# A four-layer attention and feed-forward kernel: giving up TensorE's products of the identity in banks that wait for their operands

## The chip, the cores and the metric

The kernel runs on one core of one Trainium2 chip. The metric is the time of one execution on the device in microseconds (us), from the runs of the whole program: 1483.53 us is the median of three runs before the change (1482.13 to 1483.54). Engines are named as in the profile: PE is TensorE (its weight loads are shown apart, as PEld), DVE is VectorE, ACT is ScalarE, POOL is GpSimd and SP is SyncE.

## The reference

The input is `x`, 32 sequences of 128 tokens by 128 channels, and a context of 77 rows by 128 channels for each sequence. Eight blocks follow each other, each added to the residual of a layer-normed input:

```python
x = x + _L0_xattn_ref(_layernorm(x), ctx_1024, ctx_1024, ...)   # 16 heads of 8
x = x + _L0_ffn_ref(_layernorm(x), ...)                         # 8 heads of 64, gated experts
x = x + _L1_xattn_ref(_layernorm(x), ctx_1024, 32, ...)         # the 32 largest scores of 77
x = x + _L1_ffn_ref(_layernorm(x), ...)                         # causal attention, then 8 experts, 2 chosen
x = x + _L2_xattn_ref(_layernorm(x), ctx_1024)
x = x + _L2_ffn_ref(_layernorm(x), ...)                         # quantised with the largest value of the whole x
x = x + _L3_xattn_ref(_layernorm(x), ctx_1024, ...)             # causal, 16 heads of 8
x = x + _L3_ffn_ref(_layernorm(x), ...)                         # 512 wide
```

All of it is float32, apart from the masks and the quantised products, which are bfloat16. The quantised block needs the largest value of all of `x`, and later the largest of all hidden values, so that the kernel has two points at which nothing can go on before all sequences have been seen.

## The kernel before, in words

The 32 sequences are worked in eight groups (`g`) of four. Phase A does the first five blocks for all groups; phase B the first half of the quantised block; phase C its second half and the last two blocks. In each phase every engine runs several streams of steps side by side: on TensorE of phase A the streams are `x0p`, `x0s`, `x0v` (first attention), `f0p`, `f0s`, `f0t`, `f0v`, `f0o` (first feed-forward), `x1`, `f1p`, `f1s`, `f1t`, `f1v`, `m1` (which holds the experts and the L2 attention), `kv3` and `weights`; of phase C `down`, `x3p`, `x3s`, `x3t`, `x3v` and `f3`. The order in which the streams take turns is written out as one string of letters for each phase and engine (`ORDER`), and `merge` follows it. So each engine's order is fixed when the program is built, and an engine that waits for one step holds up all the steps behind it.

TensorE writes each step's products into a PSUM bank: a ring `E` of four banks of 512 columns and a ring `S` of two pairs of banks of 1024 columns. A step takes the next bank of a ring, waits until whoever read its last contents is through (`drained`), and then waits for its operands: a copy that ACT, DVE or POOL has yet to finish. When its last product is done, the bank's `full` tells the reader.

Between these two waits stands `keep` (line 519). It looks up a digit for this use of this step in the table `FILL` (lines 93 to 151) and issues so many products of the identity with itself, 128 columns wide, into the bank that was just taken. Nobody reads them: the step's own first product starts the bank anew. No semaphore is tied to them.

```python
            def keep(o, step):
                k = uses[step] = uses.get(step, -1) + 1
                for _ in range(int(FILL[step][k])):
                    mm(o.bank[:, 0:128], ident[:], ident[:], start=True, stop=True)
```

A step that uses it, the transposes of `f0o` (from line 692):

```python
                    o = E.take("f0", g, "ys", b)
                    pe.wait_ge(o.drained, o.n)
                    keep(o, "f0o0")
                    pe.wait_ge(f0_ys, C.next(f0_ys))
                    for t in range(3):
                        ins = pe.transpose(o.bank[:, tokens(t)], ys[:, b % 2, tokens(t)], ident[:])
                    ins.then_inc(o.full, 1)
```

`FILL` has 1028 digits, of which 229 are not zero; they add up to 585. In the profile a float32 product stands as two records, so the fills are 1170 records of line 525. Of other lines that the prediction names: L530 is `transpose4`, the transposes of normed activations; L688 the second product of the first feed-forward; L826 the scores of the causal attention and L495 its masks; L840 and L672 transposes; L1197 and L1207 the two products of the last feed-forward; L2265 a product on POOL that ends a layer norm; L1219 ACT's copy out of a bank.

Of the kernel before, what the change touches and what calls it, by code (L numbers as in the profile page):

```python
# [90 lines left out]
        "fddddddfff",  # L91
}
FILL = {
    "down0": "00330000",
    "f0o0": "04000020030140000410001200000330",
    "f0o1": "00020001000010002000000000000001",
    "f0p0": "70700010",
    "f0p1": "00000000000060000000000000000000",
    "f0s0": "0000000000130300000000200001003000001000000220000003000300200000",
    "f0s1": "00000005000000003000100230301030",  # L100
    "f0t0": "2400303000000000400002003210104010001000203010000000020002000000",
    "f0v0": "00111100520002100201000000000602",
    "f1p0": "10020160",
    "f1p1": "0100000030000000",
    "f1p2": "20002040",
    "f1s0": "30000001000000002000200100037000",
    "f1t0": "00004040000000005001400302000030",
    "f1t1": "00000020000000000000000000000000",
    "f1v0": "00100002002033004000122000100333",
    "f1v1": "31012001",  # L110
    "f30": "00100009",
    "f31": "00000000000000001000000121003000",
    "f32": "00000000",
    "kv30": "00000000",
    "kv31": "00000002",
    "m10": "53015040",
    "m11": "00000000",
    "m12": "00400200",
    "m13": "1000000030000000000006203000200000000420000000020001000090000000",
    "m14": "00800027",  # L120
    "m15": "01011304",
    "m16": "10000007",
    "m17": "00000300",
    "m18": "00010008",
    "weights0": "00000001",
    "weights1": "00",
    "weights2": "0",
    "weights3": "0",
    "x0p0": "03000000",
    "x0p1": "00300200",  # L130
    "x0p2": "20000000",
    "x0p3": "00200000",
    "x0s0": "0300000000004300020020000004000000000100000130200010001000000023",
    "x0v0": "00001000300020000002110004002500",
    "x0v1": "00000000",
    "x10": "13000100",
    "x11": "00000010",
    "x12": "20030000",
    "x13": "00300001",
    "x14": "00034020",  # L140
    "x15": "71309100",
    "x16": "10011130",
    "x17": "10020011",
    "x3p0": "50000000",
    "x3p1": "05051300",
    "x3s0": "00000010000000000000000000100000",
    "x3t0": "00232020030000500000300000000200",
    "x3t1": "10000000000000030001000000000000",
    "x3v0": "00000000000100000000000000000000",
    "x3v1": "20000003",  # L150
}


# [2421 lines left out]
```

## Time and profile before

| | before |
|---|---|
| runs | 1483.53 us median of 3 (1482.13 to 1483.54) |
| the profiled execution's own time | 1494.39 us |
| its span, first to last instruction | 1492.6 us |
| granted TensorE clock, mean over the span | 0.916 |
| PE busy, with 16148 records | 1256.4 us (84%) |
| DVE / ACT / POOL busy | 1010.2 / 838.4 / 770.9 us |
| fills (L525): PE busy | 193.1 us, 1170 records |

How to read it: the profiled execution took 10.9 us longer than the median. PE's busy time is a union of records whose ends reach into the next one, so that it is more than the time in which the array works. The granted clock is 1.00 where TensorE runs at 2.4 GHz and 0.50 where it runs at 1.2 GHz; a figure between them is a mixture of the two. The chain of waits is followed back from the last instruction; on this program it reaches back to 758 us and no further, so that its shares of the span add up to about half.

### The profile page before, as it was taken

The numbers are of one execution on the slowest core, as the hardware profiler recorded it, in microseconds if no ns is written. First come the engines' busy times: TensorE is split into PE (matmuls) and PEld (weight loads), VectorE is DVE, ScalarE is ACT, GpSimd is POOL, SyncE is SP. The second block draws the span as 40 slices with busy tenths as digits, with TensorE's granted clock in tenths as the row PEclk, the third lists the DMA queues.
The fourth block names the chain that finished last, engine by engine and source line by source line (L and its number), as shares of the span: only waits on it lengthen the run. The fifth ranks groups of instructions, "written<-read, shape, count | busy, mean of one in ns | idle before, by whom it ended". The sixth has DMA issues, their size and how long they took to land. (4 is left out here: it accounts for less than half of the span.)

```text
span 1492.6 us, 40390 instructions
## 1 busy us (share of the span) xinstructions
PE 1256.4 (84%) x16148; PEld 987.0 (66%) x16149; DVE 1010.2 (68%) x2431; ACT 838.4 (56%) x2675; POOL 770.9 (52%) x793
## 2 busy tenths in 40 slices
PE   4889788878978898898899879889976678999897
PEld 3677677665756677677677757667655157776676
DVE  4357787776877786777668668887654856655562
ACT  3697666445458658658838545563544454444332
POOL 4048487475277419622853763682111677444343
PEclk8598989998989999999989889999998578999999
DMA  6000000000000000000000000001010000000000
GB/s 164 6 2 2 1 1 2 2 2 1 22 1 1 21 2 2 2 22 2 1 21 2 2 1 2 17 1 55 1 54 13 12 2 2 10 10 9 16 10 15
DMA packets 26705, 19.24 MB, mean 13 GB/s; under 512 B 6520, under 2 KB 24216, under 8 KB 26392
## 3 DMA queue, kind: packets, MB, share of 16 engines
q1 hardware_dynamic: 24936, 15.78, 3.6%
q8 instruction: 129, 2.11, 0.6%
q10 hardware_dynamic: 1584, 0.89, 0.2%
q14 instruction: 56, 0.46, 0.1%
HBM read 12.73 MB, written 3.93 MB: 11 GB/s over the span
## 5 line engine op out<-in xcount | busy, mean ns | idle before, releaser
L1219 ACT ACTIVATE arena<-bank 128x512 f32<-128x512 f32 (+5 forms) x363 | 185.8, 546 | 262.4 <-PE bank L530 90.1
L1631 DVE TENSOR_REDUCE arena<-pair 128x8 f32<-128x1024 f32 (+2 forms) x224 | 240.2, 1095 | 113.4 <-PE pair L495 59.8
L2315 POOL TENSOR_TENSOR arena<-arena 128x512 f32<-128x512 f32 x160 | 181.4, 1134 | 79.7 <-DVE arena L1749 72.7
L1266 ACT ACTIVATE arena<-pair,arena 77x128 f32<-77x128 f32 x512 | 178.3, 369 | 23.7 <-DVE arena L1631 16.9
L2320 POOL TENSOR_TENSOR arena<-arena 128x512 f32<-128x512 f32 x128 | 182.1, 1423 | 10.0
L525 PE MATMUL bank<-ident 128*128 128x128 f32 x1008 | 164.7, 299 | 9.8 <-ACT arena L1219 9.4
L525 PEld LDWEIGHTS bank<-ident 128*128 128x128 f32 x1008 | 141.5, 206 | 37.6 <-issue 18.7
L2253 POOL TENSOR_SCALAR arena<-arena 128x4 f32<-128x4 f32 x64 | 21.0, 328 | 276.6 <-DVE arena L1638 225.5
L2336 POOL TENSOR_TENSOR arena<-arena 128x512 f32<-128x512 f32 x64 | 67.4, 1070 | 136.5 <-ACT arena L1219 94.3
L2260 POOL TENSOR_SCALAR_AFFINE_SELECT arena<-arena 77x1024 f32<-77x1024 f32 x64 | 69.7, 1104 | 107.9 <-ACT arena L1603 107.8
L1603 ACT ACTIVATE arena<-pair 77x1024 f32<-77x1024 f32 x64 | 62.8, 1016 | 104.7 <-PE pair L1138 96.6
L1266 ACT ACTIVATION_READ_ACCUMULATOR arena<-pair,arena 77x1 f32 x512 | 107.9, 211 | 0.0
L1219 ACT ACTIVATE arena<-bank,arena 128x128 f32<-128x128 f32 x256 | 75.8, 509 | 40.0 <-PE bank L922 24.7
L1631 DVE TENSOR_REDUCE arena<-arena 128x4 f32<-128x32 f32 (+3 forms) x128 | 70.0, 551 | 37.0 <-ACT arena L1219 26.4
L1326 ACT ACTIVATE arena<-pair,arena 128x128 f32<-128x128 f32 x256 | 90.0, 394 | 7.6 <-DVE arena L1631 7.4
L530 PE MATMUL bank<-ident,arena 128*128 128x128 f32 (+1 forms) x352 | 59.7, 298 | 39.0 <-POOL arena L2265 17.8
L1436 ACT ACTIVATE arena<-pair 128x1024 f32<-128x1024 f32 x64 | 63.0, 1024 | 43.7 <-PE pair L495 41.8
L1784 DVE TENSOR_TENSOR arena<-bank,arena 128x512 f32<-128x512 f32 x96 | 61.3, 681 | 33.2 <-ACT arena L1219 33.1
L580 PE MATMUL pair<-arena 32*77 32x128 f32 x1024 | 74.2, 292 | 11.1 <-ACT arena L1266 9.2
L688 PE MATMUL bank<-arena 128*128 128x64 f32 x512 | 68.7, 293 | 11.4 <-ACT arena L1380 6.2
L688 PEld LDWEIGHTS bank<-arena 128*128 128x128 f32 x512 | 67.0, 210 | 16.1 <-issue 9.3
L580 PEld LDWEIGHTS pair<-arena 32*77 32x77 f32 x1024 | 59.8, 153 | 24.8 <-ACT arena L1266 11.8
(303 smaller groups left out, 2980.0 us busy)
## 6 DMA issues: line engine op xcount, KB each, us to landing
arena<-in_ctx_turned SPq DMA_DIRECT2D x16, 154.0 KB, 2.8
arena<-in_x SPq DMA_DIRECT2D x8, 256.0 KB, 4.4
out<-arena SPq DMA_DIRECT2D x8, 256.0 KB, 2.3
spill<-arena SPq DMA_DIRECT2D x7, 256.0 KB, 2.0
arena<-spill SPq DMA_DIRECT2D x7, 256.0 KB, 4.4
arena<-in_ctx SPq DMA_DIRECT2D x8, 154.0 KB
arena<-in_ctx_turned SPq DMA_DIRECT2D x1, 1232.0 KB, 5.8
wexp<-in_L_ffn_expert_w SPq DMA_DIRECT2D x1, 512.0 KB, 4.2
```

What stands on the lines that cost most here:

```text
L525: mm(o.bank[:, 0:128], ident[:], ident[:], start=True, stop=True)
L580: ins = mm(o[p].bank[0:CTX, 512 * i + 128 * j:512 * i + 128 * j + 128], sub0[rows, b, j, :], q0[rows, tokens(b)], start=True, stop=True)
L688: ins = mm(o.bank[:, h * SHD:(h + 1) * SHD], eF[:, b % 2, 512 * p + 128 * t:512 * p + 128 * t + 128], vs[:, b % 2, h, :], start=True, stop ...
L1219: return act.activation(dst, src, func, bias=bias, scale=scale)
L1266: ins = act.activation(e0[0:CTX, (2 * SEQS * g + u) % 3, tokens(i)], o.bank[0:CTX, tokens(i)], ACT.Exp, bias=negmax0[0:CTX, u, i:i + 1], a ...
L1326: ins = act.activation(pF[:, tokens(i)], o.bank[:, tokens(i)], ACT.Exp, bias=negF[:, b % 2, i:i + 1], accum_out=zF[:, b, i:i + 1])
L1436: act.activation(eG[:, (2 * SEQS * g + u) % 3, :], o.bank[:], ACT.Exp).then_inc(o.drained, 1)
L1631: return dve.tensor_reduce(dst, src, X, op, **kw)
L2260: return pool.affine_select(out=e, in_=e, compare_op=ALU.is_ge, fill=0.0, base=0, pattern=[[0, 8], [1, 128]], channel_multiplier=-1)
L2315: pool.tensor_tensor(into, xvs[:, b, ex * SHD:(ex + 1) * SHD].unsqueeze(1).broadcast_to([128, SH, SHD]), gates[g % 2][:, b, 0:SH, ex].unsq ...
L2320: ins = pool.tensor_tensor(dst, dst, into, ALU.add)
L2336: ins = pool.tensor_tensor(oprod[:, ex, :].rearrange("p (h k) -> p h k", h=SH), av, gates[g % 2][:, b, SH:, ex].unsqueeze(2).broadcast_to( ...
```

## The change

All digits of `FILL` become zero. `keep` is still called and issues nothing; the rings, the waits, the order strings and all other engines' programs are the same.

```diff
 FILL = {
-    "down0": "00330000",
-    "f0o0": "04000020030140000410001200000330",
...
-    "f0s0": "0000000000130300000000200001003000001000000220000003000300200000",
...
-    "f0t0": "2400303000000000400002003210104010001000203010000000020002000000",
...
-    "m13": "1000000030000000000006203000200000000420000000020001000090000000",
...
-    "x0s0": "0300000000004300020020000004000000000100000130200010001000000023",
...
+    "down0": "00000000",
+    "f0o0": "00000000000000000000000000000000",
...
+    "f0s0": "0000000000000000000000000000000000000000000000000000000000000000",
...
+    "f0t0": "0000000000000000000000000000000000000000000000000000000000000000",
...
+    "m13": "0000000000000000000000000000000000000000000000000000000000000000",
...
+    "x0s0": "0000000000000000000000000000000000000000000000000000000000000000",
...
 }
```

The orders of DVE, ACT, POOL and SP do not differ in a single row; TensorE's has 1674 rows before and 1438 after. In the rows that follow, a fill is an L525 row, "bank" and "pair" are the PSUM banks of the two rings, "ident" the identity, "arena" the SBUF area that holds the activations, and x9 stands for nine products of one kind in a row. First, TensorE in phase A, where the causal attention's scores of one sequence are followed by a transpose of another stream. Before:

```order
771 L826 MATMUL pair<-arena 128x256 x8
772 L495 MATMUL pair<-after,identb 32x4x32 x4
773 L495 MATMUL pair<-after,identb 32x4x64 x4
774 L495 MATMUL pair<-after,identb 32x4x96 x4
775 L495 MATMUL pair<-after,identb 32x512 x4
776 L525 MATMUL bank<-ident 128x128 x5
777 L840 MATMUL bank<-ident,arena 128x128 x2
778 L525 MATMUL bank<-ident 128x128
779 L530 MATMUL bank<-ident,arena 128x128 x4
780 L672 MATMUL bank<-ident,arena 128x128 x4
781 L525 MATMUL bank<-ident 128x128
782 L721 MATMUL bank<-arena,w1k 128x308
```

Seven fills stood here in three places between real products; after the change rows 776, 778 and 781 are gone and L840 follows L495 directly.

Second, the end of TensorE's program, where the last group's normed activations are transposed (L530) and go through the last feed-forward (L1197, L1207). The difference of the two orders:

```order
 L1164 MATMUL bank<-arena 32x128 x16
 L1164 MATMUL bank<-arena,onesd 32x128 x16
-L525 MATMUL bank<-ident 128x128 x3
 L1176 MATMUL bank<-arena 128x128 x4
-L525 MATMUL bank<-ident 128x128 x9
-L530 MATMUL bank<-ident,arena 128x128 x4
-L525 MATMUL bank<-ident 128x128 x3
+L530 MATMUL bank<-ident,arena 128x128 x4
 L1197 MATMUL bank<-arena 128x512 x4
 L1207 MATMUL bank<-arena 128x128 x16
```

Fifteen fills leave the last steps; the real products keep their order.

## Rows read from the trace of the kernel before

**Rows 1.** The page's first part, and the granted clock by core.

```profile
PE 1256.4 (84%) x16148; PEld 987.0 (66%) x16149; DVE 1010.2 (68%) x2431; ACT 838.4 (56%) x2675; POOL 770.9 (52%) x793
core 0: 1492.6 us, clock 0.916
```

**Rows 2.** Chain that ended last, by engine, as shares of the whole span.

```profile
PE 30%; DVE 6%; ACT 5%; POOL 4%; issue 3%; POOLq 0%; ACTq 0%; DVEq 0%
```

**Rows 3.** Chain of waits from 758 to 1492.6 us, shares by line.

```profile
by line: PE bank L1164 7.3%; PE bank L525 5.7%; issue 5.6%; PE pair L1138 4.6%; ACT arena L1219 4.3%; PE bank L1207 4.0%; PE bank L1197 3.6%; DVE arena L1631 3.5%; PE pair L1111 2.8%; PE bank L530 2.6%; PE pair L495 2.5%; PE pair L826 2.4%;
```

**Rows 4.** Groups by line: the fills into single banks and into pairs.

```profile
L525 PE MATMUL bank<-ident 128*128 128x128 f32 x1008 | 164.7, 299 | 9.8 <-ACT arena L1219 9.4 <-DVE arena L1906 0.3
...
L525 PE MATMUL pair<-ident 128*128 128x128 f32 x162 | 28.4, 308 | 4.8 <-DVE arena L1631 1.8 <-ACT arena L1266 1.6 <-ACT arena L1436 1.1
```

**Rows 5.** By stretch: us; busy of PE, PEld, DVE, ACT, POOL; PEclk; DMA; GB/s.

```profile
0.00:758.00 758.00, 631.77 (x7106) 506.87 (x7106) 533.99 (x1288) 485.39 (x1855) 424.81 (x431) 0.91 0.05 13
758.00:1492.60 734.60, 624.65 (x9042) 480.10 (x9043) 476.19 (x1144) 352.97 (x820) 346.09 (x363) 0.92 0.04 13
```

**Rows 6.** Busy time by stretch, line 525 alone: PE, PEld, then PEclk.

```profile
0.00:758.00 758.00, 101.88 (x622) 86.77 (x622) 0.91 0.05 13
758.00:1492.60 734.60, 91.21 (x548) 77.95 (x548) 0.92 0.04 13
```

**Rows 7.** Chain of waits from 750 to 770 us, in order of time.

```profile
758.24 2.09 PE pair L826 x16
...
760.91 2.43 PE bank L525 x10
763.35 0.43 PE bank L840 x2
```

**Rows 8.** Timeline at the program's end.

```profile
1474.47 2.17 PE L525 MATMUL bank<-ident 128*128 128x128 f32 x18
...
1478.19 1.04 POOL L2265 TENSOR_TENSOR arena<-arena 128x512 f32<-128x512 f32 x1
...
1479.28 0.65 PE L530 MATMUL bank<-ident,arena 128*128 128x128 f32 x4 [2.64 <-POOL arena L2265]
...
1480.62 3.70 PE L1197 MATMUL bank<-arena 128*128 128x512 f32 x8
...
1485.26 3.81 PE L1207 MATMUL bank<-arena 128*128 128x128 f32 x32 [0.94 <-DVE arena L2175]
```

**Rows 9.** Busy time in short stretches, all engines (columns as in rows 5).

```profile
13.70:17.10 3.40, 2.02 (x13) 1.25 (x12) 0.00 (x0) 1.30 (x4) 3.18 (x3) 1.00 0.73 144
...
212.00:215.00 3.00, 0.60 (x6) 0.41 (x4) 2.93 (x10) 2.89 (x17) 2.92 (x3) 1.00 0.00 0
218.50:222.00 3.50, 3.50 (x20) 3.27 (x21) 3.40 (x17) 0.60 (x1) 3.27 (x4) 0.51 0.00 0
222.00:225.30 3.30, 3.30 (x38) 3.00 (x38) 3.20 (x7) 0.26 (x1) 3.22 (x4) 1.00 0.00 0
...
675.90:679.30 3.40, 2.54 (x23) 2.35 (x22) 3.30 (x9) 2.84 (x16) 0.00 (x0) 1.00 0.00 0
...
1478.00:1481.40 3.40, 2.10 (x12) 1.62 (x13) 0.00 (x0) 0.60 (x1) 2.41 (x3) 1.00 0.00 0
```

**Rows 10.** The same stretches, line 525 alone: PE, PEld, then PEclk.

```profile
13.70:17.10 3.40, 0.61 (x4) 0.53 (x4) 1.00 0.73 144
143.40:146.80 3.40, 1.45 (x7) 1.16 (x6) 0.50 0.00 0
...
218.50:222.00 3.50, 2.45 (x10) 2.25 (x10) 0.51 0.00 0
675.90:679.30 3.40, 2.08 (x18) 1.96 (x18) 1.00 0.00 0
...
1245.90:1249.30 3.40, 1.22 (x4) 0.93 (x4) 0.50 0.00 0
1478.00:1481.40 3.40, 0.83 (x6) 0.75 (x6) 1.00 0.00 0
```

More of the change, by code:

```diff
@@ L93 @@
 FILL = {
-    "down0": "00330000",
-    "f0o0": "04000020030140000410001200000330",
-    "f0o1": "00020001000010002000000000000001",
-    "f0p0": "70700010",
-    "f0p1": "00000000000060000000000000000000",
-    "f0s0": "0000000000130300000000200001003000001000000220000003000300200000",
-    "f0s1": "00000005000000003000100230301030",
-    "f0t0": "2400303000000000400002003210104010001000203010000000020002000000",
[L102 to L112, printed above, removed]
+    "down0": "00000000",
+    "f0o0": "00000000000000000000000000000000",
+    "f0o1": "00000000000000000000000000000000",
+    "f0p0": "00000000",
+    "f0p1": "00000000000000000000000000000000",
+    "f0s0": "0000000000000000000000000000000000000000000000000000000000000000",
+    "f0s1": "00000000000000000000000000000000",
+    "f0t0": "0000000000000000000000000000000000000000000000000000000000000000",
+    "f0v0": "00000000000000000000000000000000",
+    "f1p0": "00000000",
+    "f1p1": "0000000000000000",
+    "f1p2": "00000000",
+    "f1s0": "00000000000000000000000000000000",
+    "f1t0": "00000000000000000000000000000000",
+    "f1t1": "00000000000000000000000000000000",
+    "f1v0": "00000000000000000000000000000000",
+    "f1v1": "00000000",
+    "f30": "00000000",
+    "f31": "00000000000000000000000000000000",
     "f32": "00000000",
     "kv30": "00000000",
-    "kv31": "00000002",
-    "m10": "53015040",
+    "kv31": "00000000",
+    "m10": "00000000",
     "m11": "00000000",
-    "m12": "00400200",
-    "m13": "1000000030000000000006203000200000000420000000020001000090000000",
[L120 to L125, printed above, removed]
+    "m12": "00000000",
+    "m13": "0000000000000000000000000000000000000000000000000000000000000000",
+    "m14": "00000000",
+    "m15": "00000000",
+    "m16": "00000000",
+    "m17": "00000000",
+    "m18": "00000000",
+    "weights0": "00000000",
     "weights1": "00",
@@ L128 @@
     "weights3": "0",
[L129 to L132, printed above, removed]
-    "x0s0": "0300000000004300020020000004000000000100000130200010001000000023",
-    "x0v0": "00001000300020000002110004002500",
-    "x0v1": "00000000",
[L136 to L150, printed above, removed]
+    "x0p0": "00000000",
+    "x0p1": "00000000",
+    "x0p2": "00000000",
+    "x0p3": "00000000",
+    "x0s0": "0000000000000000000000000000000000000000000000000000000000000000",
+    "x0v0": "00000000000000000000000000000000",
+    "x0v1": "00000000",
+    "x10": "00000000",
+    "x11": "00000000",
+    "x12": "00000000",
+    "x13": "00000000",
+    "x14": "00000000",
+    "x15": "00000000",
+    "x16": "00000000",
+    "x17": "00000000",
+    "x3p0": "00000000",
+    "x3p1": "00000000",
+    "x3s0": "00000000000000000000000000000000",
+    "x3t0": "00000000000000000000000000000000",
+    "x3t1": "00000000000000000000000000000000",
+    "x3v0": "00000000000000000000000000000000",
+    "x3v1": "00000000",
 }
```

## The prediction

> **What bounds the kernel now.** I read the page first. PE is the busiest engine, at 84% of the span with its records' overlapping ends, and none of the others is over 68%; the mean granted clock is 0.916 [rows 1]. Since the clock has two levels, 1.00 (2.4 GHz) and 0.50 (1.2 GHz), 0.084 x 2 = 16.8% of the span, 251 us, ran at 1.2 GHz. The chain by engine says who sets the pace: PE 30%, DVE 6%, ACT 5%, POOL 4%, issue 3% of the span [rows 2]. It is followed back to 758 us only, so these are parts of 48, and PE has 30 / 48, about 0.61, of the time. The kernel is thus bound by latencies in which PE has most of the links; PE's speed and PE's useless work both count at roughly six tenths. Of the later half the chain itself names the fills: L525 in single banks is 5.7% [rows 3].
>
> **What the fills cost today.** They keep PE busy for 193 us, 101.9 in the first 758 us and 91.2 after it [rows 6]. The groups show who they wait for: hardly anybody, 9.8 and 4.8 us of idle time stand ahead of them [rows 4]; a fill runs as soon as the bank is free. What matters is whether the operand behind it is still missing. Two places show both answers.
>
> - From 760.84 on, five fills (10 records) stand between the masks and L840. The chain goes straight through them: L826 2.09, fills 2.43, L840 0.43 us [rows 7]. PE was not waiting, and all 2.43 us were lost.
> - At 1474.47 nine fills take 2.17 us, and then PE still stands idle for 2.64 us, until POOL's L2265 (1.04 us from 1478.19) is done; only then can L530 start [rows 8]. POOL's layer norm hides these nine, and without them nothing moves.
>
> Sum over the later half: 5.7% of 734.6 us is 41.9 us for the single banks. Line 3 leaves the pairs out; they are 28.4 of the 193.1 us of fills [rows 4], so 41.9 / 0.85 = 49 us in all, 0.53 of the 91.2 us that fills are busy there. For the first half no chain is shown. At the same ratio it would be 54 us of 101.9; at least nothing. Other engines do more there (DVE 534 against 476, ACT 485 against 353, POOL 425 against 346 us) while PE does the same [rows 5], so I take two thirds of the ratio, 36 us. **On the path: 85 us**, and up to 103.
>
> Not all of it comes back. Each removal is a piece of 0.2 to 2.4 us, and behind it the chain turns to whoever is late next: ACT's copy (L1219), DVE's reduction (L1631), POOL. From one third to all is possible; I take two thirds, nearer to the upper end because these engines are idle for a third to a half of the span [rows 1]. **Gain: 85 x 2/3 = 57 us** (28 to 85, or 103 at the very most). Everything else about the edit is free: no semaphore, DMA or instruction of another engine is touched, and no queue is passed.
>
> **What the fills pay for.** The clock. Ahead of a fall PE did little: from 212.0 to 215.0 us it was busy for 0.60 of 3.0 us, and the clock stood at 0.51 from 215 on. In the cold stretch that follows the fills are most of what PE does, 2.45 of 3.50 us at 218.5 [rows 9, 10], and from 222.0 on the clock is at 1.00 again. Elsewhere fills keep a thin stretch at full clock: at 675.9 they are 2.08 of PE's 2.54 us, at 1478.0 0.83 of 2.10, and both stay at 1.00. Take them out, and PE has 0.5 and 1.3 us of work there, about what it had before a fall.
>
> I went through the whole span in such short stretches. Beside the 32 falls that the trace has, I find 56 stretches at 1.00 whose real work alone is as thin as that ahead of a fall, the first at 13.7 (2.02 us busy, fills 0.61) and the last at 1478.0 us, and 11 cold stretches that without fills would not have the dense work after which the clock rose, the first at 143.4 and the last at 1245.9 [rows 9, 10]. That is a count in place. Where unhidden fills go, real work moves together and some of these stretches thicken; where cold ones follow each other, there are more. I take **48 further cold stretches of 3.4 us, 163 us**, with 20 and 90 as bounds; the mean clock would fall from 0.916 to about 0.86.
>
> What one costs: at half clock PE does in 3.4 us what takes 1.7, so 1.7 us is the most. The least: with PE on 0.61 of the path and that part doubled, 3.4 us hold 3.4 / 1.61 = 2.1 us of progress, a loss of 1.3. In cold stretches PE is on the path more than on average, being slow (3.50 of 3.50 us busy at 218.5), so I take 1.5. **Cost: 48 x 1.5 = 72 us** (26 to 153).
>
> **The sum**: 1494.4 - 57 + 72 = 1509.4 us for an execution like the profiled one. That one stands 10.9 us above the median of the runs, 1483.5, so the forecast for the median is 1483.5 + 15 = **1498.5 us, slower by 1.0%**. A measurement of this kernel can tell about 0.2% from no change, 3 us; the two terms nearly cancel, and their error is several times that.
>
> The trace disagrees with one rule that would turn the sum round. It shows 16.8% of the span at 1.2 GHz with the fills in place. The Trainium skill (TensorE: Matmul & The Clock Gate, Part 1: The HAM clock gate) says of the ramp that its penalty is under 1% of a typical kernel's span and needn't be modelled; by it the second term would be at most 15 us instead of 72, and the time 1483.5 - 57 + 15 = 1441.5 us.
>
> **The rivals.**
>
> 1. *PE's relief wins: faster.* The place is the stretch from 758 us to the end, where the chain is mostly PE. If three quarters of the 85 us come back (64 us) and the work that moves together holds the clock, so that only 30 cold stretches are added at 1.3 us (39 us), the time is 1483.5 - 25 = 1458.5 us. It decides as soon as the added cold time stays under about 38 stretches at 1.5 us, the 57 us of the gain. For it: the fills on the chain are measured, the falls are not; in phase C PE's lines (L1164, L1138, L1207, L1197) lead the chain, so that it is dense anyway [rows 3]. Against it: fills make up much of PE's work just where it is thin [rows 10].
> 2. *The clock hardly counts where it falls: faster still.* Thin stretches are thin because PE waits for others. If the added cold stretches lie where POOL or DVE leads, as around 1474 to 1479 us, they cost no more than 15 us in all, and it is 1441.5 us. This is what the Trainium skill's rule of the ramp amounts to here. Against it: at the end the cold stretch reaches into L1197 and L1207, 7.5 us of PE work on the chain [rows 8].
> 3. *The clock stays down: much slower.* Without the fills that lift it out of cold stretches, cold time feeds itself: 75 further stretches at 1.5 us (112 us), and one third of the gain (28 us): 1483.5 + 84 = 1567.5 us.
> 4. *The halves cancel*, within 0.2%, 1480.5 to 1486.5 us.
> 5. *The change doesn't do what it says.* The orders exclude it: only L525 rows are gone.
>
> **How the numbers follow.** Forecast, with 1487 to 1545 us as its own range: 0.57. Rival 1: 0.21. Rival 2: 0.07. Rival 3: 0.09. Rival 4: 0.06. That gives faster 0.28, same 0.06, slower 0.66. The range runs from 1448 to 1550 us: it holds the forecast's own range, the even case and most of rival 1, and leaves out rivals 2 and 3 and the edge of rival 1.
>
> **What would show it.** In the changed kernel's profile: no L525 rows; PE busy about 1256 - 193 plus what the lower clock adds; the mean clock at 0.86 (0.90 or more speaks for rivals 1 and 2, under 0.83 for rival 3). At the end, L1197 should take clearly more than 3.7 us for its 8 records, while the last L530 still waits for POOL's L2265. L840 behind the masks should start some 2.4 us sooner after L826. If the clock falls as I say and the time falls too, the price of a cold stretch was wrong; if the clock holds, the count was.

## The result, and the profile after

| | before | after |
|---|---|---|
| median of the runs | 1483.53 us (4 runs, 1482.13 to 1484.96) | 1524.95 us (4 runs, 1522.4 to 1531.09) |
| ratio to before | | 1.0285, 95% interval 1.0253 to 1.0317 |
| profiled execution, its own time | 1494.39 us | 1524.86 us |
| its mean granted clock | 0.916 | 0.840 |
| its time at 1.2 GHz, 2 x (1 - clock) x span | 251 us | 487 us |
| its PE busy | 1256.4 us | 1200.3 us |

The change made the kernel slower by 2.85%, 41.4 us between the medians; the two profiled executions are 30.5 us apart. Forecast were 1498.5 us and 1.0%: the direction was right, the size was less than half. Two executions are left out of all ratios as slow ones, 5846.84 us of the kernel below without its exposed fills and 1500.11 us of the kernel before in the last series; nothing here explains them.

One thing must be known about the trace of before: it is of a long execution at a low clock. The kernel before ran 76 times more beside the later kernels, each time with its granted clock noted: 0.915 to 0.935, with medians of 0.922 to 0.926 by series, against 0.916 in the trace. By the medians it spends 219 to 232 us at 1.2 GHz, not 251, so that a later kernel's trace held against this one makes its loss of clock look some 20 to 30 us of cold time too small.

The page after, its first part and the chain by engine, and the granted clock by core:

```profile
PE 1200.3 (79%) x14978; PEld 900.5 (59%) x14979; DVE 1005.3 (66%) x2431; ACT 838.3 (55%) x2675; POOL 770.0 (51%) x793
...
PE 25%; DVE 10%; ACT 5%; POOL 4%; issue 4%; POOLq 0%; DVEq 0%; ACTq 0%
```

```profile
core 0: 1523.1 us, clock 0.840
```

Beside [rows 1, 2] the reader sees three things. PE has 1170 records less, yet is busy for only 56 us less, where the fills alone were 193 us: the rest of its work got slower. The other engines' busy time has not moved. And on the chain DVE went from 6% to 10% of the span, PE from 30% to 25%.

The two halves, to be held against [rows 5]:

```profile
0.00:762.00 762.00, 595.71 (x6414) 455.88 (x6415) 525.97 (x1274) 480.91 (x1844) 414.17 (x420) 0.84 0.05 13
762.00:1523.10 761.10, 604.61 (x8566) 444.58 (x8565) 479.31 (x1157) 357.35 (x834) 355.87 (x374) 0.84 0.04 12
```

The clock falls from 0.91 to 0.84 in the first half and from 0.92 to 0.84 in the second: it is no matter of one stage.

The place of [rows 7] after the change, TensorE's timeline (start, duration, what, and in brackets the idle time before it with who ended it) and the chain there:

```profile
771.07 1.15 PE L826 MATMUL pair<-arena 32*128 32x256 f32 x16 [3.21 <-DVE arena L1631]
772.15 0.45 PE L495 MATMUL pair<-after,identb 32*32 32x128 bf16 x16
772.52 0.69 PE L840 MATMUL bank<-ident,arena 128*128 128x128 f32 x2
```

```profile
771.52 2.29 DVE arena L1790
...
774.97 1.22 DVE arena L1631
```

The same timeline of before, for comparison:

```profile
758.24 2.09 PE L826 MATMUL pair<-arena 32*128 32x256 f32 x16 [2.54 <-DVE arena L1631]
760.26 0.65 PE L495 MATMUL pair<-after,identb 32*32 32x128 bf16 x16
760.84 2.50 PE L525 MATMUL bank<-ident 128*128 128x128 f32 x10
763.14 0.63 PE L840 MATMUL bank<-ident,arena 128*128 128x128 f32 x2
```

L840 follows the masks at once, 1.45 us after L826's start instead of 4.90 us. Of these 3.45 us the fills are 2.30; the rest is L826 and the masks, which the clock, at 1.2 GHz here before, now runs mostly at 2.4 GHz. But the chain no longer goes through PE: it goes through DVE's L1790 and L1631. L826 itself waits 3.21 us for DVE, where it had waited 2.54 us before. The relief is there, and it is partly turned into waiting.

The end of the program, to be held against [rows 8]:

```profile
1507.27 1.09 PE L530 MATMUL bank<-ident,arena 128*128 128x128 f32 x4 [4.74 <-POOL arena L2265]
1509.13 5.66 PE L1197 MATMUL bank<-arena 128*128 128x512 f32 x8 [0.78 <-ACT arena L1219]
1515.73 3.81 PE L1207 MATMUL bank<-arena 128*128 128x128 f32 x32 [0.94 <-DVE arena L2175]
```

L530 still waits for POOL's L2265, 4.74 us instead of 2.64 with nine fills (2.17 us) ahead of it: these fills had been hidden. L1197 now takes 5.66 instead of 3.70 us, at a mean clock of 0.65, so that about 4 us of it ran at 1.2 GHz.

### Where the time went: the two traces side by side

Since TensorE's real products stand in the same order in both kernels, their starts can be compared one by one. From each product to the next I took the time in the trace of before and in the other trace, and added up the differences in three piles: pairs of neighbours with a fill between them in either kernel; pairs without one whose first product ran at different clocks in the two; and the rest, which is mostly waiting. A pile moves by one to three us with how the clock of a product is told.

| us, against the trace of before | with fills between | clock differs | the rest | sum |
|---|---|---|---|---|
| after | -85.1 | +79.4 | +36.4 | +30.7 |

The 85.1 us are the fill time that left PE's path. 36.4 us of it came back as waits for others. The net relief is thus some 49 us, and the lower clock took some 79 us, against this trace of before.

### The profile page after: what moved, and what is told of

Read it like the earlier page. It is cut to its first block and busy times, and to the rows that moved or that the text cites. A ratio compares the mean times of both kernels' runs of the same rounds, so it can differ in the third digit from the quotient of the medians.

```text
span 1523.1 us, 38155 instructions
## 1 busy us (share of the span) xinstructions
PE 1200.3 (79%) x14978; PEld 900.5 (59%) x14979; DVE 1005.3 (66%) x2431; ACT 838.3 (55%) x2675; POOL 770.0 (51%) x793
## 5 line engine op out<-in xcount | busy, mean ns | idle before, releaser
L1631 DVE TENSOR_REDUCE arena<-pair 128x8 f32<-128x1024 f32 (+2 forms) x224 | 240.1, 1095 | 132.7 <-PE pair L495 64.4
L530 PE MATMUL bank<-ident,arena 128*128 128x128 f32 (+1 forms) x352 | 64.9, 316 | 66.3 <-POOL arena L2265 26.0
L1631 DVE TENSOR_REDUCE arena<-arena 128x4 f32<-128x32 f32 (+3 forms) x128 | 70.0, 551 | 44.9 <-ACT arena L1219 33.9
L580 PE MATMUL pair<-arena 32*77 32x128 f32 x1024 | 82.4, 316 | 16.1 <-ACT arena L1266 13.2
L530 PEld LDWEIGHTS bank<-ident,arena 128*128 128x128 f32 (+1 forms) x352 | 44.9, 161 | 83.2 <-issue 74.7
L922 PE MATMUL bank<-wexp,arena 128*128 128x512 f32 x128 | 78.2, 734 | 12.4 <-DVE arena L1946 9.7
L580 PEld LDWEIGHTS pair<-arena 32*77 32x77 f32 x1024 | 66.9, 169 | 31.5 <-ACT arena L1266 16.5
L688 PE MATMUL bank<-arena 128*128 128x64 f32 x512 | 73.5, 306 | 13.2 <-DVE arena L1774 7.5
L688 PEld LDWEIGHTS bank<-arena 128*128 128x128 f32 x512 | 71.8, 223 | 19.0 <-issue 12.8
```

The costliest lines, as they stand in the source:

```text
L530: ins = pe.transpose(o.bank[0:cols, b * rows:(b + 1) * rows], src[:, b, :], ident[0:rows, 0:rows])
L580: ins = mm(o[p].bank[0:CTX, 512 * i + 128 * j:512 * i + 128 * j + 128], sub0[rows, b, j, :], q0[rows, tokens(b)], start=True, stop=True)
L688: ins = mm(o.bank[:, h * SHD:(h + 1) * SHD], eF[:, b % 2, 512 * p + 128 * t:512 * p + 128 * t + 128], vs[:, b % 2, h, :], start=True, stop ...
L922: mm(o.bank[:, 0:512], nTm[:, tokens(b)], wexp[:, 512 * i:512 * i + 512], start=True, stop=True)\
L1631: return dve.tensor_reduce(dst, src, X, op, **kw)
```

## The experiments

Theory 1: fills cost the time that they are on the path and pay through the clock; the change lost more clock than it gained path. Theory 2: the loss has nothing to do with the clock. All ratios are to the kernel before on the same chip.

### Same time, a small corner of the array: the price of the clock alone

```diff
-                    mm(o.bank[:, 0:128], ident[:], ident[:], start=True, stop=True)
+                    mm(o.bank[0:32, 0:128], ident[0:32, 0:32], ident[0:32, :], start=True, stop=True)
```

> All 585 fills stay at their places, but each multiplies only the 32 x 32 corner of the identity with 32 rows of it, still 128 columns long: TensorE is occupied about as long as by the full fill, with a sixteenth of the array. Theory 1 (the fills pay through the clock, and what they take is a price): the clock falls as it did without fills, to about 0.84, and the time of the fills stays, so that it is slower than before and than the change: 1483.5 + about 84 us = 1567 us (1550 to 1580). Theory 2 (what the change lost is not the clock but the spacing that the fills gave to TensorE's order): the same as before, 1480 to 1490 us.

1584.59 us, ratio 1.0638 (1.0602 to 1.0674), clock 0.844. The groups of fills in its trace, to be held against [rows 4], and the clock:

```profile
L525 PE MATMUL bank<-ident 32*32 32x128 f32 x1008 | 170.6, 306 | 8.0 <-ACT arena L1219 7.6 <-DVE arena L1906 0.3
...
L525 PE MATMUL pair<-ident 32*32 32x128 f32 x162 | 27.7, 302 | 3.8 <-ACT arena L1266 1.8 <-ACT arena L1436 1.4 <-DVE arena L1631 0.4
```

```profile
core 0: 1584.4 us, clock 0.844
```

The small fills take what the full ones took (198 against 193 us busy) and stand at the same places, but the clock is where it is with no fills at all. So the kernel keeps the price and loses what it was paid for. This run takes the two terms of the prediction apart. **The clock**: 0.0638 x 1483.5 = 95 us (89 to 100), for 494 - 251 = 243 us more at 1.2 GHz between the two traces, and 495 - 232 = 263 us more between the medians of the executions. By the medians a microsecond at 1.2 GHz costs 95 / 263 = 0.36 us. **The relief**: from here to the changed kernel, 1.0638 to 1.0285, 0.0353 x 1483.5 = 52 us. The time is 5 us above the range that Theory 1 gave; Theory 2, 1480 to 1490 us, is out, and so is any rival in which the clock hardly counts. The small fills differ from the full ones in their rows, in their columns of the array and in how many of their operands are zero; no run takes these apart.

### Hidden and exposed fills apart

In the trace of before I sorted the 229 places by whether PE was idle behind the fills (for over 0.08 us), or their operand was ready earlier: 108 places with 319 fills as mostly hidden, 121 with 266 as mostly exposed. The sorting has a fault that I saw only afterwards: all 81 fills into pairs of banks came out as hidden, though the products behind them start 0.1 to 0.2 us later than a fill's length even where nothing is waited for. So the 266 are exposed, but up to 81 of the 319 are too. Each of two kernels has one kind emptied; of one step, before, with the first kind alone, and with the second alone:

```diff
-    "m10": "53015040",
+    "m10": "00000040",
...
-    "m10": "53015040",
+    "m10": "53015000",
```

> Of 229 places the 121 whose fills (266) were mostly on the path of TensorE in the trace of before are emptied; the 108 places (319 fills) with TensorE idle behind them stay. Theory 1 with relief and clock of about equal size: 67 us of exposed fill time go, of which six tenths come back (40 us); 266 / 585 of the clock's loss comes (38 us): 1475 to 1490 us, clock about 0.88. Theory 1a (only the hidden fills hold the clock where it is about to fall, since idle time is what makes it fall): clock still about 0.90, time 1445 to 1465 us. Theory 2: slower than before by roughly half of the change, 1500 us.

1487.87 us, ratio 1.0005 (0.9974 to 1.0036), clock 0.902. No difference from before, with 266 fills fewer. The time fits Theory 1, and the clock, about 0.90, Theory 1a; neither had both.

> The complement: only the 121 places with exposed fills (266) stay, the 108 hidden ones (319 fills) are emptied. Theory 1: nothing comes back, since the removed ones were hidden, and 319 / 585 of the clock's loss comes: 1483.5 + 46 = 1530 us, clock about 0.87. Theory 1a: nearly all of the clock's loss comes: 1555 to 1570 us, clock about 0.85. Theory 2: about 1484 us, since hidden fills space nothing.

1518.67 us, ratio 1.0199 (1.0165 to 1.0233), clock 0.873. The 319 fills are worth 2.0%, about 30 us net, of the 46 us that Theory 1 gave; Theory 1a's 1555 to 1570 us is out. Together with the first kernel's nothing this makes 2.0 of the change's 2.85%. The clock has the difference: by the medians the first kernel spends 59 us more at 1.2 GHz than before, the second 154 us, and the changed one 257 us, more than both together.

The first of the two leaves two readings: the exposed fills neither cost nor bring anything, or both are equal. One more kernel tells them apart, with all 585 fills, of which the exposed 266 multiply the 32 x 32 corner:

```diff
+                    if THIN[step][k] == "1":
+                        mm(o.bank[0:32, 0:128], ident[0:32, 0:32], ident[0:32, :], start=True, stop=True)
+                    else:
+                        mm(o.bank[:, 0:128], ident[:], ident[:], start=True, stop=True)
```

> All 585 fills stay; the 266 mostly exposed ones multiply only a 32 x 32 corner (same length, a sixteenth of the array), the 319 hidden ones are full. e3_hidden, which empties those 266, took the time of before, either since they neither cost nor bring anything, or since their cost and the clock that they hold are equal. Equal and opposite: slower than before by what the relief of e3_hidden was, 30 to 40 us: 1515 to 1525 us, clock 0.90. Neither: 1484 to 1490 us.

1521.64 us, ratio 1.0246 (1.0208 to 1.0283), clock 0.903. Equal and opposite: full instead of small, the exposed fills hold clock worth 36 us (0.0246 x 1483.5); small instead of none, they cost the same, (1.0246 - 1.0005) x 1483.5 = 36 us. It also tests the price: by the medians this kernel spends 318 - 223 = 95 us more at 1.2 GHz than before, and 95 x 0.36 = 34 us. The kernel without these fills spends only 59 us more there, so that of the 36 us between the two some 13 are clock again and some 23 the path. The page of the kernel without exposed fills shows where their relief goes:

```profile
PE 25%; DVE 10%; ACT 5%; POOL 4%; issue 4%; DVEq 0%; ACTq 0%; POOLq 0%
```

PE is at 25% of the chain and DVE at 10%, as after the change, at nearly the clock of before.

### The end of the program alone

```diff
-    "f30": "00100009",
+    "f30": "00100000",
-    "f31": "00000000000000001000000121003000",
+    "f31": "00000000000000001000000121000000",
-    "x3v1": "20000003",
+    "x3v1": "20000000",
```

> Only the last 15 fills go, those ahead of L1176, L530 and L1197 of the last group; 570 stay. Theory 1: nine of them are hidden behind POOL's layer norm, and without them the clock is down when L1197 (3.70 us before for 8 records) and perhaps L1207 (3.81 us) run; 3 to 5 us slower, L1197 at 7 us. Theory 2: no difference beyond the six short fills on the path, 0 to 1 us faster.

1488.03 us, ratio 1.0009 (0.9991 to 1.0028): by the whole time it can't be told from no change, nor from a loss of 2.4 us. Its trace tells more:

```profile
1458.06 1.13 PE L1176 MATMUL bank<-arena 128*128 128x128 f32 x8 [1.50 <-DVE arena L2159]
1463.93 1.08 PE L530 MATMUL bank<-ident,arena 128*128 128x128 f32 x4 [4.75 <-POOL arena L2265]
1465.79 5.46 PE L1197 MATMUL bank<-arena 128*128 128x512 f32 x8 [0.78 <-ACT arena L1219]
1472.19 3.81 PE L1207 MATMUL bank<-arena 128*128 128x128 f32 x32 [0.94 <-DVE arena L2175]
```

From L1176's start to L1207's end these are 17.9 us. In the trace of before L1176 starts at 1473.50 and L1207 ends at 1489.07, 15.6 us. So the last 15 fills are worth 2.4 us in this stretch, somewhat less than the 3 to 5 us expected: L1197 goes back to full clock halfway (5.46, not 7 us). The six short fills, which the expectation had on the path, were not on it either: L1197 starts 1.86 us after L530 instead of 1.34, since L530 is slower (1.08 against 0.65 us) and L1197 then waits 0.78 us for ACT's copy, and L1176 waits 1.50 us for DVE, where it had waited 0.63 us behind 0.94 us of fills.

### Amount or place

The digits of each step are shuffled among that step's uses; the number of fills stays at 585.

> All 585 fills, but the digits of each step are shuffled among the uses of that step: the amount stays, the place changes. Theory 1 with place: fewer of them fall into thin stretches and more onto the path; between the change and no change or above it, 1500 to 1540 us, clock 0.86 to 0.89. Theory 3 (only the amount of work on TensorE counts): 1480 to 1490 us, clock 0.915.

1562.6 us, ratio 1.0507 (1.0455 to 1.0559), clock 0.885. Slower than without any fill, and beyond my range. The same number at other places holds half as much clock: by the medians 358 us at 1.2 GHz, where the kernel before has 226 and the changed one 489. And the step-by-step comparison has +44.2 us between neighbours with fills, where the change has -85.1: more of them landed on the path. The place decides whether fills gain or lose; Theory 3 is out.

### Fills in cold stretches

Emptied are only the 20 places (59 fills) that ran at 1.2 GHz in the trace of before.

> Only the 59 fills at 20 places that ran while the clock was at 1.2 GHz in the trace of before are emptied; 526 stay. In that trace cold stretches with many fills were followed by full clock. If these fills lift the clock: longer cold stretches, 10 to 20 further ones for 59 fills, a loss of 13 to 26 us less 10 us of relief: 1487 to 1502 us. If they only take time at the slow clock: 12 us of them come back, 1472 to 1480 us.

1492.66 us, ratio 1.0046 (1.002 to 1.0071), clock 0.908. In the step-by-step comparison 16.2 us came back between neighbours with fills, and still the kernel is 7 us slower: by the clock 2 x (1 - 0.908) x 1492.3 = 275 us ran at 1.2 GHz instead of 251 (by the medians 261 instead of 223). So these fills do shorten the cold time, as far as the sum goes. The single place that I had named for it doesn't show it. Around [rows 9]'s 218.5 the answers for this kernel are (columns as in rows 5):

```profile
215.00:218.50 3.50, 0.83 (x6) 0.66 (x5) 3.40 (x12) 3.38 (x20) 3.34 (x4) 0.92 0.00 0
218.50:222.00 3.50, 3.50 (x20) 3.38 (x21) 3.36 (x27) 1.73 (x9) 3.27 (x4) 0.50 0.00 0
222.00:225.30 3.30, 3.30 (x25) 3.08 (x24) 3.27 (x10) 0.09 (x1) 3.06 (x4) 0.58 0.00 0
```

Clocks of 0.92, 0.50 and 0.58 are 0.6 + 3.5 + 2.8 = 6.9 us of cold time, as long as the one before from 215 to 222, without the five fills ahead of L658. At this place the real products went without those five fills and the cold time was no longer; why is not shown.

### Phase C alone

> Only the fills of phase C go (78 fills at 30 places; steps down, x3 and f3), phases A and B keep theirs. In the comparison of the two traces, step by step, the lag of the change behind before stands at 29 us when phase C begins and at 30.5 us at the end; so phase C's share of the change is about nothing: 1480 to 1487 us. By the shares of the chain alone, some 24 us of fills busy there would give back 8 to 14 us: 1470 to 1477 us.

1487.42 us, ratio 0.9995 (0.9962 to 1.0029), clock 0.915. Phase C's 78 fills bring nothing net, within 0.3%. But that is again two equal terms and not none: by the medians this kernel spends 258 us at 1.2 GHz where the kernel before beside it spends 226, 32 us more, and at 0.36 that is 12 us. So by this estimate, good to about half of itself, a relief of some 12 us was there, in the 8 to 14 us that the chain's shares promised, and the clock took it. The trace alone hides this (clock 0.915 against 0.916), since that of before is of a cold execution.

### Looking for a version that beats both

Four kernels were to use the finding. None did. Three add fills to idle time; the table's `m10`, for example, in the first, where the exposed fills are gone as well, and in the third:

```diff
-    "m10": "53015040",
+    "m10": "00000049",
...
-    "m10": "53015040",
+    "m10": "53015049",
```

> The hidden 319 fills of e3_hidden stay, and at every place where TensorE was still idle in that run's trace between the free bank and its operand, as many more are added as fit into the idle time (0.235 us each, 0.2 us left over): 739 fills at 209 places, none meant to be on the path. If the two halves of theory 1 hold together (hidden fills cost nothing and hold the clock; exposed ones cost their time), the relief of some 40 us stays and the clock is back at 0.93 or more: 1435 to 1460 us. If fills in idle time are not free (they delay what comes after them once times shift), 1480 to 1500 us at a clock of 0.93.

1505.77 us, ratio 1.0131 (1.0095 to 1.0168), clock 0.920. The clock is back, the time isn't. The groups of its fills:

```profile
L525 PE MATMUL bank<-ident 128*128 128x128 f32 x1056 | 156.6, 294 | 5.5 <-POOL subscale L2206 4.3 <-ACT arena L1219 0.9 <-DVE arena L1906 0.3
...
L525 PE MATMUL pair<-ident 128*128 128x128 f32 x422 | 67.4, 298 | 40.4 <-DVE arena L1631 18.5 <-ACT arena L1436 10.8 <-ACT arena L1603 7.9
```

Part of it is a fault of my construction, which the second line shows. The steps `f1s`, `f1t`, `x3s` and `x3t` take two pairs of banks at once, and `keep` stands behind the waits for both; I had reckoned the idle time from when the first was free. So their fills (142, where the base had 28) start behind the late pair, after 40.4 us of idle time in all, and are probably on the path from the first to the last: by this estimate 114 x 0.22 = 25 us, more than the 1.3%. Without them the time would be about that of before, not the 1435 to 1460 us. What properly hidden fills would have done here stays open.

> The 319 hidden fills of e3_hidden, and 154 more at the 41 places close ahead of a fall of the clock or inside a cold stretch of that run's trace where TensorE was idle between the free bank and its operand (473 in all). If aimed fills hold the clock without delaying much: clock 0.93, 1460 to 1480 us, faster than both kernels. If, as in e5_waits, fills that were to be hidden slip onto the path once times shift: 1485 to 1500 us.

1498.28 us, ratio 1.009 (1.0059 to 1.0121), clock 0.906. The same fault put 34 of the 154 added fills on the path, by the same estimate 7.5 us of the 13 us. The clock rose from 0.902 to 0.906 only (medians 0.902 and 0.908): fills aimed at the falls of one trace held little of the next one's clock.

> The kernel before with 141 more fills at 34 places chosen in the same way from its own trace (726 in all), so that the base is as it was. Aimed fills hold: clock 0.94 or more, 1465 to 1480 us. They slip: 1490 to 1510 us.

1492.37 us, ratio 1.006 (1.0034 to 1.0087), clock 0.929. Here 20 of 141 are misplaced, 4.4 us of the 9. By the medians the clock rose from 0.925 to 0.931, 17 us less at 1.2 GHz, worth 6 us; the added fills took more than twice that.

The fourth takes fills away where TensorE's real work is thickest; `f0p0` for example:

```diff
-    "f0p0": "70700010",
+    "f0p0": "70700000",
```

> Of the exposed fills of the kernel before, only the 106 at 53 places go around which TensorE's real work alone stays well above what it had ahead of a fall of the clock; 479 stay. If the count by thin stretches tells which fills hold the clock: 24 us of exposed time go, six tenths come back, and the clock stays above 0.91: 1465 to 1476 us, faster than both kernels. If times shift so that other stretches turn thin: 1482 to 1492 us at a clock of 0.90.

1490.53 us, ratio 1.0048 (1.0022 to 1.0074), clock 0.912. In the step-by-step comparison 27.7 us came back between neighbours with fills, waits took 22.6 us of it, and 1.1 us went to the clock: its trace is 4 us shorter than the trace of before, while by the twelve runs it is 7 us slower. The medians explain it: 255 us at 1.2 GHz against 219 of the kernel before beside it, 36 us more, worth 13 us, less the net relief of some 5 us, gives the 7 or 8 us. Times did shift, and the clock that the 106 fills had held was lost.

All kernels by this account (each against the kernel before beside it; the third column is the second times 0.36; "left" is what the fills themselves cost or give back):

| | more at 1.2 GHz, medians | worth | measured | left |
|---|---|---|---|---|
| the change: no fills | +257 us | +92 | +42 | -50 |
| all small | +263 us | +95 | +95 | 0 (sets the price) |
| exposed ones small | +95 us | +34 | +36 | +2 |
| without the exposed | +59 us | +21 | +1 | -20 |
| without the hidden | +154 us | +55 | +30 | -25 |
| without phase C's | +32 us | +12 | -1 | -13 |
| without those in cold stretches | +38 us | +14 | +7 | -7 |
| without 106 exposed ones | +36 us | +13 | +7 | -6 |
| without the last 15 | -1 us | 0 | +1 | +1 |
| shuffled | +132 us | +48 | +75 | +27 |
| hidden ones and 420 more (739) | -6 us | -2 | +19 | +21 |
| hidden ones and 154 more (473) | +53 us | +19 | +13 | -6 |
| all and 141 more (726) | -17 us | -6 | +9 | +15 |

For the change, whose runs had no kernel before with noted clocks beside them, 232 us are taken, as for the small fills. The price is from one kernel; that it fits the exposed ones made small, where the fills' own time also stays, is its only check, and the other rows are worked out with it.

## Why the prediction was right or wrong

**The sign** was right, and by the mechanism of the forecast: fewer fills, lower clock, slower products on a path that PE leads. Rivals 1, 2 and 4 are out by the time, and rival 2 by its mechanism too. The price of the clock is measured by itself at 95 us (89 to 100), where rival 2, and with it the Trainium skill's rule of a ramp under 1% of the span (TensorE: Matmul & The Clock Gate, Part 1: The HAM clock gate), gave 15 at most; the trace has 32% of the span at 1.2 GHz. The page gives that figure for the ramp of a typical kernel, not for a clock that keeps falling as it does here (33 cold stretches before the change, 47 after), so that the rule was no ground for rival 2. Rival 3's 75 further cold stretches came true nearly to the number (257 / 3.4 = 76 by the medians), its low relief and its price didn't.

**The relief** was right: forecast 57 us, measured 52. Its parts agree: 85 us on the path, against 85.1 us between neighbours with fills (the nearness is luck, one being a chain's share and the other a difference), and two thirds of it recovered, against (85.1 - 36.4) / 85.1 = 0.57. What takes it back is DVE's L1790 and L1631 at the place looked at; DVE's reduction was the second of the three that the forecast named.

**The step that failed** is "48 further cold stretches of 3.4 us, 163 us". Measured are 487 - 251 = 236 us between the two traces, 69 such stretches, and 489 - 232 = 257 us by the medians, 76 of them; with the small fills it is 263 us. The count in place had been 56 and 11, 67 in all, and I cut it to 48 because real work would move together where unhidden fills go. The sum shows that the cut was wrong; that the plain count comes close is in part luck. Product by product, 313 us of the cold time after fall on products that ran at full clock before, while 61 us that were cold before ran at full clock after, and of the count's own examples the first, 13.7 us, stayed at 1.00. A likely reason is that 36.4 of the 85.1 us came back as waits, idle time that keeps stretches thin; no run shows that by itself. The second factor was too high: 95 / 263 x 3.4 = 1.2 us for a stretch, against 1.5, and even under the 1.3 that the prediction took as the least. Its 0.61 for PE's share of the path is a slip, by the way (30 / 48 is 0.63), and changes none of this. Together 72 us became 95 with the fills kept small, and 42 + 52 = 94 in the change itself.

**The sum**: 95 - 52 = 43 us against 72 - 57 = 15. The clock term's 23 us and the relief's 5 make up the difference. Where each term is a difference between larger things, a quarter's error in one was more than the result.

**The places**: L840 behind the masks came sooner, as said; L1197 took longer, 5.66 us, as said; the mean clock was to be 0.86 and is 0.840. "PE busy about 1256 - 193 plus what the lower clock adds" holds with 137 us for the latter. "L840 some 2.4 us sooner" was 3.45, of which 2.30 are the fills. That both halves of the kernel share the loss was not said.

## What to carry to other kernels

Work whose result nobody reads can pay for itself on TensorE, but only where it stands: the same 585 products at shuffled places cost 5%, at the chosen places they bring 2.8%. Before judging such an edit, take its two terms apart with one kernel that keeps the fills' time and drops what holds the clock (a small corner of the array, the same number of columns); the difference to either side is then each term by itself. Where an edit "does nothing", look at the clock as well: four kernels here stood within 0.5% of before with 32 to 59 us more at 1.2 GHz, and a relief that paid for half to all of it. Compare clocks by the medians of many executions and not by one trace. And when an estimate discounts a plain count by an argument, give the plain count a weight of its own unless a row shows the discount.

## What the runs showed of the hardware that I had not expected

- Products that occupy TensorE as long as full ones (mean 306 against 299 ns a record in single banks) but use 32 rows and 32 columns of the array hold no clock at all: 0.844, against 0.840 with none and 0.916 with full ones. How long PE is busy (1377.7 us here, the most of all kernels) doesn't tell the clock. In this kernel PE is busy without a gap from 131.6 to 158.9 us, and the granted clock stays at 0.50:

```profile
131.60:158.90 27.30, 27.30 (x207) 21.53 (x205) 15.38 (x27) 17.49 (x89) 21.56 (x20) 0.50 0.01 2
```

  Whether it is the rows, the columns or the values that count, no run separates.
- A microsecond at 1.2 GHz costs 0.36 us in this kernel with all fills small and 0.38 us (36 / 95) with the exposed ones small; 0.5 us would be the cost if PE were on the path all the time. Among the kernel before's own executions, unchanged, those with less clock are the slower ones as well, by 0.2 to 0.4 us for each microsecond, by series.
- The clock alone doesn't tell the time. 726 fills gave a median clock of 0.931 against 0.925 before, and are 0.6% slower.
